# A hash-routed expert stage on one core: one flat loop over full tiles with copied weights, and slots of 40 rows for what is left

## The chip, the cores and the metric

One core of one Trainium2 chip runs the whole kernel. The metric is device time in microseconds (us) for one execution, lower is better. All arithmetic of the part that changes is float32.

## The reference, cut to what matters

2048 tokens (4 sequences of 512) of width 128 go through an attention block with a layernorm, and then through eight experts of hidden width 512. Which experts a token gets is a hash of its own first two values:

```python
h = jnp.mod(x_flat[:, :2].sum(axis=1).astype(jnp.int32), E)      # E = 8
sel = jnp.stack([h, jnp.mod(h + 1, E)], axis=1)
# for every expert e, and only for tokens with e in sel:
y = jnp.maximum(x_flat @ W1e + b1e, 0.0) @ W2e + b2e
acc += 0.5 * y
x = layernorm(x + acc)
```

So a token of group h needs experts h and h+1, and nothing else. With the inputs of setup_inputs, evaluating the reference's first half and its hash puts 1052, 324, 132, 35, 10, 29, 131 and 335 tokens into groups 0 to 7.

## The kernel before, in words

The core's engines are programmed one by one and meet through semaphores.

**Attention.** A loop over t = 0..18 (16 token tiles of 128 and a pipeline of three) computes attention on TensorE, ScalarE and VectorE. The normalised rows (x1, with the token's own index as a 129th value) are scattered by GpSimd's indirect DMA (line 514) into a DRAM array `groups`, in one segment for each group (`seg` in the code). In front of each segment lie 128 rows of padding whose index is out of range.

**Full tiles.** As soon as the first 12 token tiles are counted, VectorE computes on one row (full_tiles and full_rows, lines 920 to 944) the first FULL = 5 tiles that are certainly full, with their expert and start row (full_table). They run as five unrolled steps j = 0..4. SyncE reads their table entries into registers (load_table, line 306), and starts a DMA for the first-layer weights w1f (line 352, into a ring of three) and for the rows xrow (line 362). TensorE turns the rows (columns, line 1299), multiplies up (line 1308) and down (line 1323), ScalarE applies bias and relu (line 680, with biases b1x that VectorE picked) and copies the sum out (fsum, line 727). The second layer's weights are read from w2_s at an offset held in a register.

**Remaining tiles.** After the last tokens are placed, VectorE counts each group's remaining tiles (count_tiles, lines 956 to 971): at least one for each group. Then every engine runs eight loops, one for each group e, whose bounds come from tile_table. In each iteration k:
- SyncE waits for `kept` and `xT_up`, and fetches 128 rows twice: xs (line 387, to be turned) and xrow (line 388, for the residual).
- TensorE: up with expert e into bA (4 products of 128x128x128), up with expert e+1 into bB and bC (4 more), down with expert e (line 1452), the turn of the next tile's rows (columns, line 1303), down with expert e+1 (line 1459). Each float32 product is two instructions. Weights are read in place from w1_s and w2_s at fixed offsets.
- ScalarE: 4 relus for ha and 2 for hb (line 680). VectorE: the other 2 relus for hb (line 1077), the copy xsT (line 1051), the previous tile's finish (line 1045, which waits for the store before it), then ysum (1027), y2 (1032), bn_stats (1034) and bn_aggr (1037).
- GpSimd: the deviation (lines 557 and 559), the index copy (563) and the indirect store of the tile (567), one at a time: the copy waits until the store before it has landed.

A last tile of a group that is not full is run as a full tile of 128 rows, whose leading rows are done twice or are padding.

## Time and profile before

| | us |
|---|---|
| median of 3 runs | 238.8 (237.17 to 240.47) |
| the profiled execution, own time | 238.23 |
| its span in the trace | 236.5 |
| TensorE busy in the span | 212.2 (90%) |
| VectorE, ScalarE, GpSimd busy | 147.3, 120.6, 117.8 |

The profiled execution's own time is 1.73 us above its span: what lies around the traced instructions. Times in the rows below count from the span's start. "Idle before" names what ended an engine's wait. A chain of waits is followed back from the last instruction of the kernel.

### The profile page before, as it was taken

Reading aid. Unit: us, or ns where it says so; the run is one execution under the profiler, and the core shown is the slowest. Engines: PE = TensorE matmul, PEld = TensorE weight load, DVE = VectorE, ACT = ScalarE, POOL = GpSimd, SP = SyncE. Lnnn points to the kernel's source line nnn. Section 1 sums busy time; section 2 is a strip of 40 time slices with the busy share of each in tenths; the row PEclk is TensorE's granted clock in tenths of the full one; section 3 lists DMA queues with packets and bytes.
Section 4 is the critical chain, followed back from the end, with each engine's and each line's share of the span. In section 5 each row is a group of like instructions: output and inputs, shape, how many; then the busy total and the mean of one; then the engine's idle time right before and its main releaser. Section 6 shows DMA issues by size and latency. Waiting matters only on the chain.

```text
span 236.5 us, 10737 instructions
## 1 busy us (share of the span) xinstructions
PE 212.2 (90%) x4009; PEld 176.2 (75%) x4009; DVE 147.3 (62%) x521; ACT 120.6 (51%) x360; POOL 117.8 (50%) x219
## 2 busy tenths in 40 slices
PE   6879999999998999998999988999999999999920
PEld 2445778767777667886776678989999999899920
DVE  6836448585877765888898616734655555555540
ACT  3546557765466646765656145754344434344400
POOL 6563034852544427762647601847646545455541
PEclk9999999999999999999999999999999999999995
DMA  4131120112232132130001365212121212121100
GB/s 100 58 94 47 49 96 3 45 52 91 91 78 66 47 103 72 43 96 15 28 25 36 117 201 151 96 38 76 40 62 44 56 43 57 27 48 36 35 22 7
DMA packets 18557, 14.73 MB, mean 62 GB/s; under 512 B 2647, under 2 KB 15547, under 8 KB 18513
## 3 DMA queue, kind: packets, MB, share of 16 engines
q1 hardware_dynamic: 17008, 11.83, 17.9%
q0 software_dynamic: 1216, 2.16, 2.8%
q8 instruction: 30, 0.49, 0.9%
q10 hardware_dynamic: 288, 0.13, 0.3%
q14 instruction: 15, 0.11, 0.2%
HBM read 11.43 MB, written 3.03 MB: 61 GB/s over the span
## 4 chain that ended last, share of the span: by engine, by line
PE 74%; DVE 6%; issue 5%; DMA 4%; POOL 3%; ACT 3%; SPq 1%; POOLq 0%; ACTq 0%; DVEq 0%
PE bS L1308 12%; PE bT L1251 7%; PE bV L1452 6%; PE bV L1459 5%; PE bS L1194 4%; PE bV L1266 4%; PE bS L1219 4%; PE bJ L1170 3%; PE bV L1323 3%; PE bT L1308 3%; PE bS L1233 2%; PE bL L1367 2%; PE bS L1201 2%; PE bV L1274 2%; DMA out<-yo,idx 2%
## 5 line engine op out<-in xcount | busy, mean ns | idle before, releaser
L680 ACT ACTIVATE ha<-bS,b1c 128x128 f32<-128x128 f32 x68 | 19.4, 368 | 38.0 <-PE bS L1308 38.0
L668 ACT COPY PTs<-bT 128x512 f32<-128x512 f32 (+3 forms) x48 | 25.9, 539 | 18.2 <-PE bT L1251 18.2
L567 POOL DMA_INDIRECT out<-yo,idx x18 | 19.4, 1076 | 17.5 <-POOL idx L563 9.6
L1251 PE MATMUL bT<-ident,Pr 128*128 128x128 f32 x168 | 27.2, 277 | 0.5 <-issue 0.4
L1308 PE MATMUL bS<-xsT,w_s 128*128 128x128 f32 x204 | 26.3, 279 | 1.1 <-issue 1.0
L1308 PEld LDWEIGHTS bS<-xsT,w_s 128*128 128x128 f32 x204 | 24.1, 192 | 2.2 <-issue 2.2
L498 POOL TENSOR_SCALAR rstd<-mv 128x1 f32<-128x1 f32 x16 | 3.8, 236 | 44.0 <-DVE mv L859 44.0
L1251 PEld LDWEIGHTS bT<-ident,Pr 128*128 128x128 f32 x168 | 19.5, 141 | 5.4 <-issue 4.1
L514 POOL DMA_INDIRECT groups<-x,pos x16 | 16.5, 1034 | 11.7 <-DVE pos L909 8.4
L655 ACT ACTIVATE Pr<-bS 128x512 f32<-128x512 f32 x32 | 20.1, 629 | 3.0 <-PE bS L1233 3.0
L814 DVE TENSOR_REDUCE mx<-bS 128x8 bf16<-128x512 f32 x32 | 21.4, 677 | 0.0
L819 DVE TENSOR_REDUCE mx<-bS 128x8 bf16<-128x128 f32 (+3 forms) x16 | 7.9, 491 | 20.6 <-issue 14.9
L1459 PE MATMUL bV<-w_s,hb 128*128 128x128 f32 x136 | 18.5, 277 | 0.0
L1452 PE MATMUL bV<-w_s,ha 128*128 128x128 f32 x136 | 18.1, 276 | 0.2 <-DVE ysum L1027 0.2
L1077 DVE TENSOR_SCALAR hb<-bT,b1c 128x128 f32<-128x128 f32 x34 | 10.5, 347 | 11.7 <-PE bT L1308 11.0
L1459 PEld LDWEIGHTS bV<-w_s,hb 128*128 128x128 f32 x136 | 16.7, 191 | 0.3
L1452 PEld LDWEIGHTS bV<-w_s,ha 128*128 128x128 f32 x136 | 16.5, 192 | 0.4 <-ACT ha L680 0.4
L1266 PE MATMUL bV<-Vx,PTs 128*32 128x18 f32 x1024 | 15.2, 186 | 1.3 <-DVE rem L835 0.8
L1266 PEld LDWEIGHTS bV<-Vx,PTs 128*32 128x32 f32 x1024 | 12.4, 111 | 4.5 <-issue 3.2
L631 ACT COPY Vx<-bJ 64x256 f32<-64x256 f32 x32 | 12.0, 374 | 7.0 <-PE bJ L1170 6.8
L504 POOL TENSOR_SCALAR x<-y,mv,rstd 128x128 f32<-128x128 f32 x15 | 13.0, 867 | 1.6
L559 POOL TENSOR_TENSOR rstd<-rstd,half 128x1 f32<-128x1 f32 x22 | 12.5, 567 | 1.7
(237 smaller groups left out, 496.9 us busy)
## 6 DMA issues: line engine op xcount, KB each, us to landing
w_s<-in_L_ffn_W SPq DMA_DIRECT2D x16, 256.0 KB
w1f<-in_L_ffn_W SPq DMA_DIRECT2D x10, 256.0 KB, 3.0
xrow<-groups SPq DMA_DIRECT2D x22, 64.5 KB, 1.9
xs<-groups SPq DMA_DIRECT2D x18, 64.0 KB
x_tok<-in_L_attn_x SPq DMA_DIRECT2D x4, 256.0 KB, 3.7
groups<-padrows SPq DMA_DIRECT2D x1, 516.0 KB, 6.0
b2r<-in_L_ffn_b SPq DMA_DIRECT2D x1, 512.0 KB, 3.4
out<-yo,idx POOLq DMA_INDIRECT x18
```

Source lines behind the costliest of these rows:

```text
L504: nc.gpsimd.tensor_scalar(x1[:, t, 0:D], y[:, q, :], mv[:, q, 0:1], rstd[:, q, :], ALU.subtract, ALU.mult).then_inc(ln_done, 1)
L514: nc.gpsimd.indirect_dma_start(seg, bass.IndirectOffsetOnAxis(ap=pos[:, t:t + 1], axis=0), x1[:, t, :], None).then_inc(done, 16)
L567: nc.gpsimd.indirect_dma_start(rows_out, bass.IndirectOffsetOnAxis(ap=idx[:], axis=0), yo[:, FULL - 1, :], None, bounds_check=T * P - 1, o ...
L655: nc.scalar.activation(Pr[:, t % 2, j, :].rearrange("p (z c) -> p z c", z=2), own[j], ACT.Exp, scale=SCALE).then_inc(exped[j], 1)
L668: nc.scalar.copy(PTs[:, j, 0:m, :], bT[:, 0:m * P].rearrange("p (c q) -> p c q", c=m)).then_inc(turned_out, 1)
L680: nc.scalar.activation(dst[:, c, :], src[:, c * P:(c + 1) * P], ACT.Relu, bias=bias_of(c)).then_inc(relu, 1)
L814: nc.vector.tensor_reduce(mx[:, j, :].rearrange("p (z h) -> p z h", z=2), own[j].rearrange("p z (h k) -> p z h k", h=4), AX.X, ALU.max).th ...
L1251: last = nc.tensor.transpose(bT[:, c * P:(c + 1) * P], Pr[:, t % 2, j, c * P:(c + 1) * P], ident[:])
L1266: last = mm(bV[i * W:(i + 1) * W, a * PW:(a + 1) * PW], PTs[:, j, c, i * W:(i + 1) * W], Vx[:, q, i, a, :], start=True, stop=True)
L1308: last = mm(bank_of(c)[:, c * P:(c + 1) * P], w[:, c * P:(c + 1) * P], xsT[:], start=True, stop=True)
L1452: mm(bY[:, 0:D], ha[:, c, :], w2_s[:, e, c, :], start=(c == 0), stop=False)
L1459: last = mm(bY[:, 0:D], hb[:, c, :], w2_s[:, a, c, :], start=False, stop=(c == FC - 1))
```

## The change

A group's rest of up to TS = 40 rows is no longer a tile. Each group has a slot of 40 rows (its last 40), and three slots share one tile xt (GT = 3, TT = 3). Tiles beyond the five full ones are those that a group needs for all but such a rest. They run in one loop k = FULL..last on every engine, with expert and row read from a table in each iteration. TensorE reads its weights from four fixed buffers w1a, w1b, w2a and w2b; ScalarE copies the next tile's weights into them (128x512 float32 each). All of hb's relus move to VectorE. xb = 0.5 b2 + x is made ahead of the sum. The table (count_tiles) has an entry for each tile and is computed by a longer row of small VectorE operations on one partition; full_biases is gone and biases are read at an offset in a register. w1_s and w2_s have a ninth expert, a copy of the first.

After the loop come eight passes, one for each expert, in the order 1, 2, 3, 0, 4, 5, 6, 7: 80 columns (the slots of the two groups that use the expert) go up and down with weights of 64 columns, the sums gather transposed in three banks that begin with the second layer's biases, and are turned back, normalised and stored in three tiles of up to 120 rows.

At the end of attention the order on TensorE changes: the last token tile's turn (attT) is no longer behind columns(0) and up_full(0, 0). In SyncE's program, ahead of the loop's first fetch, stand now: eight table reads for the slots, two for the table, four DMAs of 256 KB for the first tile's weights, and eight DMAs for the slots' rows.

The diff, cut to its core:

```diff
+    TS = 40
+    GT = P // TS
+    TT = -(-E // GT)
+    LAST = (T * P + E * (P - TS - 1)) // P
+    NT2 = LAST - FULL
+    ENTRIES = NT2 + 1
+    SLOTS = LAST + 1
+    ORDER = [1, 2, 3, 0, 4, 5, 6, 7]
...
@@ SP @@
+                    if e <= E:
+                        sp.dma_start(w1_s[:, e, :], W1[e % E]).then_inc(f_in, 16)
+                        sp.dma_start(w2_s[:, e, :, :], W2[e % E].rearrange("(c p) d -> p c d", p=P)).then_inc(f_in, 16)
...
+            def load_tile(k, row):
+                sp.wait_ge(kept, k * 16)
+                sp.wait_ge(xT_up, k)
+                sp.dma_start(xs[:], seg[bass.ds(row, P), 0:D]).then_inc(tile_in, 16)
+                sp.dma_start(xrow[:, bass.ds(k * XW, XW)], seg[bass.ds(row, P), :]).then_inc(kept, 16)
+            tail = load_table(sp, tail_table, range(E), tails_ok, E * SEG - TS)
+            last = load_bound(sp)
+            e = load_table(sp, table[:, 0, :], [1], table_ok, E - 1)[0]
+            for s, w1_to, w2_to in ((0, w1a, w2a), (1, w1b, w2b)):
+                a = (e + s) % E
+                sp.dma_start(w1_to[:].unsqueeze(1),
+                             W1[bass.ds(a, 1)].rearrange("e p f -> p e f")).then_inc(first_in, 16)
+                sp.dma_start(w2_to[:].rearrange("p (c d) -> p c d", c=FC),
+                             W2[bass.ds(a, 1)].rearrange("e (c p) d -> p (e c) d", p=P)).then_inc(first_in, 16)
             sp.wait_ge(scattered_late, 16 * KT_)
-            for e in range(E):
-                if e > 0:
-                    tail += load_table(sp, tail_table, [e], tails_ok, E * SEG - P)
-                    first += load_table(sp, tile_table[:, 0, :], [e + 1], table_ok, T + E, FULL)
-                with sp.Fori(first[e], first[e + 1]) as k:
-                    i = nc.s_assert_within(k - first[e], 0, T - 1,
-                                           skip_runtime_bounds_check_because="a group has at most all T tiles")
-                    row = nc.s_assert_within(tail[e] - i * P, 0, E * SEG - P,
-                                             skip_runtime_bounds_check_because="rows of no token precede a group's")
-                    sp.wait_ge(kept, k * 16)
-                    sp.wait_ge(xT_up, k)
-                    sp.dma_start(xs[:], seg[bass.ds(row, P), 0:D]).then_inc(tile_in, 16)
-                    sp.dma_start(xrow[:, bass.ds(k * XW, XW)], seg[bass.ds(row, P), :]).then_inc(kept, 16)
-            sp.wait_ge(xT_up, first[E])
+            for g in range(E):
+                h = (g % GT) * TS
+                sp.dma_start(xt[h:h + TS, g // GT, :], seg[bass.ds(tail[g], TS), :]).then_inc(tail_in[g // GT], 16)
+            with sp.Fori(FULL, last) as k:
+                at = entry_of(k)
+                load_tile(k, sp.value_load(table[0:1, bass.ds(at, 1), 0:1].rearrange("a n c -> a (n c)"),
+                                           min_val=0, max_val=E * SEG - P))
+            sp.wait_ge(xT_up, last)
...
@@ GpSimd @@
+            tail_deviation(0)
+            pool.wait_ge(out_in, last * 16)
+            tail_deviation(1)
+            tail_store(0)
+            tail_deviation(2)
+            tail_store(1)
+            tail_store(2)
             pool.wait_ge(table_ok, 1)
-            pool.wait_ge(out_in, first[E] * 16)
+            pool.wait_ge(out_in, last * 16)
+            pool.wait_ge(tail_stored, 16 * TT)
...
@@ ScalarE @@
+            columns_copy(0)
+            act.wait_ge(b1c_ok, 1)
+            def bias_of(e):
+                return lambda c: b1c[:, bass.ds(e * FC + c, 1)]
+            def bias_at(e):
+                return lambda c: b1c[:, e * FC + c:e * FC + c + 1]
+            relus(ha, bA, 0, up_a, bias_of(experts[0]), FC)
...
+            for t in range(TT):
+                n = len(groups_of(t))
+                act.wait_ge(tail_up, t + 1)
+                nc.scalar.copy(xTt[:, t * GT:t * GT + n, :],
+                               slot_turn[t][:, 0:n * TS].rearrange("p (g r) -> p g r", g=n)).then_inc(tail_out, 1)
+            act.wait_ge(down, FULL)
+            nc.scalar.copy(fsum[:, HEAD, :], bY[:, 0:D]).then_inc(f_out, 1)
+            w1v = w1_s[:].rearrange("p e f -> p (e f)")
+            w2v = w2_s[:].rearrange("p e c d -> p (e c d)")
+            last = load_bound(act)
+            act.wait_ge(f_in, 32 * (E + 1))
+            with act.Fori(FULL, last) as k:
+                e, after = load_experts(act, k)
+                act.wait_ge(up_a, k + 1)
+                act.wait_ge(full_ok, 1)
+                for c in range(FC):
+                    nc.scalar.activation(ha[:, c, :], bA[:, c * P:(c + 1) * P], ACT.Relu,
+                                         bias=bias_of(e)(c)).then_inc(relu, 1)
+                act.wait_ge(full_ok, 1)
+                nc.scalar.copy(w1a[:], w1v[:, bass.ds(after * F, F)]).then_inc(w1a_ok, 1)
+                act.wait_ge(up_b, k + 1)
+                act.wait_ge(full_ok, 1)
+                nc.scalar.copy(w1b[:], w1v[:, bass.ds(after * F + F, F)]).then_inc(w1b_ok, 1)
+                act.wait_ge(half_down, k + 1)
+                act.wait_ge(full_ok, 1)
+                nc.scalar.copy(w2a[:], w2v[:, bass.ds(after * F, F)]).then_inc(w2a_ok, 1)
+                act.wait_ge(down, k + 1)
+                act.wait_ge(full_ok, 1)
+                nc.scalar.copy(w2b[:], w2v[:, bass.ds(after * F + F, F)]).then_inc(w2b_ok, 1)
+            for i, e in enumerate(ORDER):
+                h, src = slot_hidden[i % 3]
+                act.wait_ge(slot_up, i + 1)
+                if i >= 3:
+                    act.wait_ge(slot_down, i - 2)
+                for c in range(FC):
+                    nc.scalar.activation(h[:, c, 0:2 * TS], src[:, c * 2 * TS:(c + 1) * 2 * TS], ACT.Relu,
+                                         bias=bias_at(e)(c)).then_inc(slot_relu, 1)
...
@@ VectorE @@
+            with dve.Fori(HEAD, last1) as last:
+                k = last + 1
+                e = load_experts(dve, k)[0]
+                dve.wait_ge(up_b, k + 1)
+                dve.wait_ge(down, k)
+                for c in range(FC):
+                    nc.vector.tensor_scalar(hb[:, c, :], bB[:, c * P:(c + 1) * P],
+                                            b1c[:, bass.ds(e * FC + FC + c, 1)], 0.0, ALU.add, ALU.max).then_inc(relu_b, 1)
+                column_copy(k + 1)
+                dve.wait_ge(out_in, last * 16)
+                dve.wait_ge(rs_ok, k)
+                finish(FULL - 1)
+                dve.wait_ge(kept, k * 16 + 16)
+                dve.wait_ge(y_ok, k)
+                nc.vector.scalar_tensor_tensor(xb[:], b2f[:, bass.ds(e * D, D)], 0.5, xrow[:, bass.ds(k * XW, D)],
+                                               ALU.mult, ALU.add).then_inc(xb_ok, 1)
+                dve.wait_ge(down, k + 1)
+                dve.wait_ge(xb_ok, k + 1)
+                nc.vector.scalar_tensor_tensor(y2[:, FULL - 1, :], bL[:, 0:D], 0.5, xb[:], ALU.mult,
+                                               ALU.add).then_inc(y_ok, 1)
+                moments(k, FULL - 1)
...
+            tail_flatten(0)
+            tail_moments(0)
+            tail_finish(0)
+            tail_flatten(1)
+            tail_moments(1)
+            tail_flatten(2)
+            tail_moments(2)
+            tail_finish(1)
+            tail_finish(2)
...
@@ TensorE @@
-                if t == T + 2:
-                    keep_busy(6)
-                    columns(0)
-                    keep_busy(4)
-                    up_full(0, 0)
-                    pe.wait_ge(f_in, 32 * E)
-                    experts = load_table(pe, full_table[:, 0, :], [0, 1], full_ok, E - 1)
-                if t > T:
-                    keep_busy(6 if t == T + 1 else 2)
                 if t >= 3:
                     pe.wait_ge(gated, t - 2)
                     nc.tensor.transpose(aT, att[:], ident[:]).then_inc(attT_up, 1)
+                if t == T + 2:
+                    columns(0)
                 if t < T:
                     score_rows(t)
-                if t == T + 2:
-                    up_full(0, 1)
-                if t == T + 1:
+                if t >= T + 1:
...
+            pe.wait_ge(f_in, 32 * (E + 1))
+            experts = load_table(pe, experts1, [0, 1], full_ok, E - 1)
+            up_full(0, 0)
+            up_full(0, 1)
...
+            for t in range(TT):
+                n = len(groups_of(t)) * TS
+                pe.wait_ge(tail_in[t], 16 * len(groups_of(t)))
+                nc.tensor.transpose(slot_turn[t][:, 0:n], xt[0:n, t, 0:D], ident[0:n, 0:n]).then_inc(tail_up, 1)
+            pe.wait_ge(summed, T)
+            pe.wait_ge(first_in, 64)
+            with pe.Fori(FULL, last) as k:
+                pe.wait_ge(w1a_ok, k + 1)
+                up(lambda c: bA, k, w1a, up_a)
+                pe.wait_ge(w1b_ok, k + 1)
+                up(lambda c: bB, k, w1b, up_b)
+                pe.wait_ge(y_ok, k)
+                pe.wait_ge(w2a_ok, k + 1)
+                by_act = k * FC + FULL * FC
+                for c in range(FC):
+                    pe.wait_ge(relu, by_act + c + 1)
+                    i = mm(bL[:, 0:D], ha[:, c, :], w2a[:, c * P:(c + 1) * P], start=(c == 0), stop=False)
+                i.then_inc(half_down, 1)
+                columns(k + 1)
+                pe.wait_ge(w2b_ok, k + 1)
+                for c in range(FC):
+                    pe.wait_ge(relu_b, k * FC + c + 1)
+                    i = mm(bL[:, 0:D], hb[:, c, :], w2b[:, c * P:(c + 1) * P], start=False, stop=(c == FC - 1))
+                i.then_inc(down, 1)
+            HF = P // 2
...
+                dst = slot_hidden[i % 3][1]
+                if i >= 3:
+                    pe.wait_ge(slot_relu, FC * (i - 2))
+                if e == 0:
+                    cols = xTt[:, 0:E:E - 1, :]
+                else:
+                    cols = xTt[:, e - 1:e + 1, :].rearrange("p g r -> p (g r)")
+                for c in range(FC):
+                    for h in range(2):
+                        to = dst[h * HF:(h + 1) * HF, c * 2 * TS:(c + 1) * 2 * TS]
+                        last_up = mm(to.rearrange("p (g r) -> p g r", g=2) if e == 0 else to,
+                                     w1_s[:, e, c * P + h * HF:c * P + (h + 1) * HF], cols, start=True, stop=True)
+                last_up.then_inc(slot_up, 1)
...
+                groups = (0, E - 1) if e == 0 else (e - 1, e)
+                parts = [(groups[0], 0), (groups[1], 1)] if e % GT == 0 else [(groups[0], 0)]
+                for c in range(FC):
+                    pe.wait_ge(slot_relu, FC * i + c + 1)
+                    for g, q in parts:
+                        n = TS if len(parts) == 2 else 2 * TS
+                        at = (g % GT) * TS
+                        for h in range(2):
+                            last_down = mm(slot_sum[g // GT][h * HF:(h + 1) * HF, at:at + n],
+                                           w2_s[:, e, c, h * HF:(h + 1) * HF], hid[:, c, q * TS:q * TS + n],
+                                           start=False, stop=False, skip_group_check=True)
+                last_down.then_inc(slot_down, 1)
...
+            for i in range(E + 2):
+                if i < E:
+                    slot_pass_up(i)
+                if i >= 2:
+                    slot_pass_down(i - 2)
+                while back < TT and i - 3 >= max(ORDER.index((g + s) % E) for g in groups_of(back) for s in range(2)):
+                    turn_back(back)
+                    back += 1
```

## Rows read from the trace of the kernel before

**Rows 1.** The page: busy time of each engine.

```profile
PE 212.2 (90%) x4009; PEld 176.2 (75%) x4009; DVE 147.3 (62%) x521; ACT 120.6 (51%) x360; POOL 117.8 (50%) x219
```

**Rows 2.** Window from the loops' first to their last product: us, busy of each engine, clock.

```profile
159.70:226.40 66.70, 65.26 (x561) 63.34 (x560) 37.98 (x137) 28.14 (x102) 36.85 (x72) 1.00 0.19 47
```

**Rows 3.** The page: loop tiles' relus (four each).

```profile
L680 ACT ACTIVATE ha<-bS,b1c 128x128 f32<-128x128 f32 x68 | 19.4, 368 | 38.0 <-PE bS L1308 38.0
```

**Rows 4.** Chain of waits, loop tiles, TensorE: start us, us, what.

```profile
183.33 1.34 PE bS L1308 x12
...
187.01 1.34 PE bS L1308 x12
```

**Rows 5.** Timeline: TensorE's pair of table reads, the last token tile's sum, the first loop tile's turn.

```profile
138.91 0.39 PE L1281 MATMUL bJ<-spare 128*128 128x256 bf16 x2 [0.62 <-issue]
...
140.57 0.29 DVE L855 TENSOR_TENSOR y<-bL,x_tok 128x128 f32<-128x128 f32 x1 [4.43 <-PE bL L1367]
...
157.97 0.27 PE L1303 MATMUL bS<-ident,xs 128*128 128x128 f32 x1
```

**Rows 6.** Timeline of SyncE's DMA issues before the loops and at the first tile.

```profile
143.26 3.23 SPq L352 DMA_DIRECT2D w1f<-in_L_ffn_W  x4
153.96 0.33 SPq L387 DMA_DIRECT2D xs<-groups  x1
154.50 0.35 SPq L388 DMA_DIRECT2D xrow<-groups  x1
```

**Rows 7.** Chain of waits: SyncE's table reads ahead of its first DMAs, and a landing.

```profile
130.83 0.47 SPq L306
...
132.16 0.02 SPq L306
...
133.86 2.48 DMA xrow<-groups
```

**Rows 8.** Timeline of VectorE: a turn of the loop without, then one with a table read.

```profile
173.55 0.18 DVE L1037 BATCH_NORM_AGGREGATE mv<-st 128x2 f32<-128x6 f32 x1
...
174.04 0.61 DVE L1077 TENSOR_SCALAR hb<-bT,b1c 128x128 f32<-128x128 f32 x2 [0.30 <-issue]
...
196.36 0.18 DVE L1037 BATCH_NORM_AGGREGATE mv<-st 128x2 f32<-128x6 f32 x1
197.46 0.61 DVE L1077 TENSOR_SCALAR hb<-bT,b1c 128x128 f32<-128x128 f32 x2 [0.92 <-PE bT L1308]
197.98 0.28 DVE L1051 COPY xsT<-bS 128x128 f32<-128x128 f32 x1
198.18 0.34 DVE L1045 TENSOR_SCALAR yo<-y,mv,rstd 128x128 f32<-128x128 f32 x1
...
199.26 0.29 DVE L1032 SCALAR_TENSOR_TENSOR y<-ysum,xrow 128x128 f32<-128x128 f32 x1
199.58 0.29 DVE L1034 BATCH_NORM_STATS2 st<-y 128x6 f32<-128x128 f32 x1
```

**Rows 9.** Timeline of ScalarE: two 128x512 operations in a row; the relus of a loop tile.

```profile
124.47 0.63 ACT L655 ACTIVATE Pr<-bS 128x512 f32<-128x512 f32 x1
...
124.96 0.63 ACT L659 ACTIVATE Pr<-bS 128x512 f32<-128x512 f32 x1
...
184.26 1.14 ACT L680 ACTIVATE ha<-bS,b1c 128x128 f32<-128x128 f32 x4 [2.03 <-PE bS L1308]
```

**Rows 10.** Timeline: weight loads of 128 and of 32 columns, and products on the latter.

```profile
122.32 0.71 PE L1170 MATMUL bJ<-wvg,xT 128*32 128x64 f32 x32 [0.28 <-ACT ranks L623]
...
122.78 0.43 PEld L1266 LDWEIGHTS bV<-Vx,PTs 128*32 128x32 f32 x32
...
181.16 0.97 PEld L1452 LDWEIGHTS bV<-w_s,ha 128*128 128x128 f32 x8
```

**Rows 11.** Timeline: last products and last store of the kernel.

```profile
225.27 1.06 PE L1459 MATMUL bV<-w_s,hb 128*128 128x128 f32 x8
...
230.59 1.05 POOL L567 DMA_INDIRECT out<-yo,idx  x1 [0.85 <-POOL idx L563]
```

More of the change, by code:

```diff
@@ L306, in load_table, with load_bound, entry_of, load_experts @@
             return [eng.value_load(tab[0:1, i:i + 1], min_val=least, max_val=most) for i in entries]
+        rows1, experts1 = table1[:, 0, :], table1[:, 1, :]
+        def load_bound(eng):
+            return load_table(eng, bound_table, [0], table_ok, LAST, FULL + 1)[0]
+        def entry_of(k):
+            return nc.s_assert_within(k - FULL, 0, NT2 - 1,
+                                      skip_runtime_bounds_check_because="the loop ends at the table's last entry")
+        def load_experts(eng, k):
+            at = entry_of(k)
+            return [eng.value_load(table[0:1, bass.ds(at, 1), i:i + 1].rearrange("a n c -> a (n c)"),
+                                   min_val=0, max_val=E - 1) for i in (1, 2)]
+        def groups_of(t):
+            return range(t * GT, min((t + 1) * GT, E))
         def expand(eng, dst, src, mask, n):
@@ L701, in _ @@
                 if t == T + 1:
-                    columns_copy(0)
+                    for s in (w1a_ok, w1b_ok, w2a_ok, w2b_ok):
+                        act.sem_inc(s, FULL + 1)
+                    act.sem_inc(half_down, FULL)
+                    experts = load_table(act, experts1, [0, 1], full_ok, E - 1)
                 if 1 <= t <= T:
@@ L727, in _ @@
                     nc.scalar.copy(fsum[:, j, :], bY[:, 0:D]).then_inc(f_out, 1)
[L728 removed]
+            relus(hb, bB, HEAD, up_b, bias_of(experts[HEAD] + 1), FC // 2)
             columns_copy(FULL)
[L730 to L740 removed]
+            relus(hb, bB, HEAD, up_b, bias_of(experts[HEAD] + 1), FC, FC // 2)
@@ L956, in count_tiles @@
[L956 to L970 removed]
+                n = FULL
@@ new lines, in full_rows @@
+                ends = spread(upto[:, Z + 1:], n)
+                row, expert = found1[:, 0, :], found1[:, 1, :]
+                link(nc.vector.tensor_tensor(reached[:, 0:n, :], ends, along(0, n), ALU.is_le))
+                nc.vector.tensor_reduce(expert, reached[:, 0:n, 0:E - 1], AX.X, ALU.add)
+                link(nc.vector.tensor_tensor(cover[:, 0:n, :], reached[:, 0:n, :], ends, ALU.mult))
+                link(nc.vector.tensor_reduce(gone[:], cover[:, 0:n, :], AX.X, ALU.max))
+                link(nc.vector.scalar_tensor_tensor(row, gone[:], -float(P), jrow[:, 1, 0:n], ALU.mult, ALU.add))
@@ new lines, in _ @@
+            pe.wait_ge(b2q_in, 16)
+            pe.wait_ge(share_ok, 1)
+            pe.wait_ge(f_out, FULL)
+            pe.wait_ge(tail_out, TT)
+            for t in range(TT):
+                slot_biases(t)
+            pe.wait_ge(xT_out, last + 1)
+            back = 0
+            for i in range(E + 2):
[6 more added lines that the diff above has]
+                    back += 1
```

383 lines of the change are left out of this document (213 added, 170 removed).

## The prediction

> **What bounds the kernel now.** I read the page's busy times first: TensorE is busy for 90% of the span, nobody else for over 62% [rows 1]. Then the stretch that the change rewrites, the loops over the remaining tiles. It is 66.7 us long, TensorE is busy for 65.3 us of it at the full granted clock (1.00, the 2.4 GHz level), ScalarE for only 28.1 us and VectorE for 38.0 us [rows 2]. So the loops are TensorE's. How many tiles? ScalarE does 68 relus into ha, four for each tile: 17 tiles [rows 3]. 66.7 / 17 = 3.92 us each. In the chain of waits one undisturbed tile follows the other after 187.01 - 183.33 = 3.68 us [rows 4]; the 0.24 us on top are turns of loops and changes of expert.
>
> **What the change removes.** By the reference the groups hold 1052, 324, 132, 35, 10, 29, 131 and 335 tokens. Five full tiles come from group 0. Before, the rest needs 4+3+2+1+1+1+2+3 = 17 tiles, which the trace bears out. After, a group needs ceil((n-40)/128) tiles in all: 3+3+1+0+0+0+1+3 = 11 in the loop. Six tiles go, 6 x 3.92 = 23.5 us. Four things pay for that, in the order of time.
>
> **Step A: the loop starts later.** In the five unrolled steps TensorE turns the first loop tile's rows inside the last step, at 157.97, and the loops start 1.73 us later, at 159.70 [rows 2, 5]. After the change TensorE gets to the last token tile's projection before it multiplies the first full tile, which brings that tile's sum (140.57 [rows 5]) some 3 us forward, and with it the placing. But SyncE's program decides when the rows of the first loop tile come, and SyncE works without a pause there: the last four DMAs of full-tile weights end at 143.26 + 3.23 = 146.5 [rows 6]. Behind them now stand:
> - ten table reads. Two of SyncE's take from 130.83 to 132.18, 1.35 us [rows 7]; TensorE does a pair in 0.62 us [rows 5]. I take 0.6 us for one, nearer to SyncE's own row: 6.0 us, with 3.1 and 6.8 us as ends;
> - four DMAs of 256 KB, at most 3.23 / 4 = 0.8 us each, of which part is table reads; I take 0.6: 2.4 us;
> - eight slot DMAs, each at the pitch of two neighbours, 154.50 - 153.96 = 0.54 us [rows 6]: 4.3 us;
> - one more table read for the tile's row, 0.6 us, and the landing: a fetch of the same size took 2.48 us on the chain [rows 7], I take 2.2.
> Sum: 146.5 + 6.0 + 2.4 + 4.3 + 0.6 + 2.2 = 162.0, and 0.5 for the loop's entry and the waits: 162.5. TensorE would be ready for it near 156, so it stands idle for over 6 us, and all small savings ahead of it (the earlier last tile, full_biases gone, register offsets for relus that are slower) fall into that hole and are worth nothing. The static part ends at 162.5 + 1.7 = 164.2. Ends: 161 and 166.
>
> **Step B: a tile of the flat loop.** TensorE still has the same 32 instructions and one turn, 3.68 us at least. Two others now have more than that.
> - VectorE. From the start of hb's two relus to xsT it takes 0.52 us, so 0.26 for one [rows 8]; four are 1.04. xsT to yo is 0.20; yo, then xb, then y2 0.44 each way as from one 128x128 operation with a semaphore to the next (estimate from yo's own 0.34 and the 0.1 around it): 0.85. y2 to bn_stats is 0.32 [rows 8], to bn_aggr 0.40. From bn_aggr to the next relu a plain turn takes 174.04 - 173.55 = 0.49 us, one with a table read and a change of loop 197.46 - 196.36 = 1.10 [rows 8], so a read costs up to 0.6; with two reads in each turn I take 1.5. Sum: 1.04 + 0.20 + 0.85 + 0.32 + 0.40 + 1.5 = 4.31 us.
> - ScalarE. Four relus 1.14 [rows 9]. A copy of 128x512 from SBUF is not in the trace; the nearest rows, from PSUM, take 0.63 each and start 0.49 apart [rows 9], so four are 1.96 to 2.5. The last copy waits for the tile's last product; from there 1.5 us for turn and reads (as for VectorE, part of it beside the copy), 1.14 of relus, 0.3 until the first half's last pair is through, 1.0 for the turn and the second half: 4.0 to 4.1 us from product to product.
> I take 4.3 us, VectorE's sum; 3.92 (TensorE's mean of before) and 5.15 are the ends, the latter worked out below. Entry: TensorE turns the slots, ScalarE copies them (three times), copies fsum, reads the bound and the first entry before the first relu: 1.4 us more than in a steady turn. 164.2 + 1.4 + 11 x 4.3 = 212.9.
>
> **Step C: the slots' passes.** Each product of float32 is two instructions. Up: 8 passes x 4 x 2 halves x 2 = 128. Down: five passes of 16 and three (experts 0, 3, 6, whose two slots lie in different banks) of 32 = 176. Together 304, with weights of 64 columns. Weight loads of 128 columns come 0.97 / 8 = 0.121 us apart, those of 32 columns, in turn over four column strips, 0.43 / 32 = 0.013; products of 64 columns on the latter 0.71 / 32 = 0.022 [rows 10]. There is no row for 64 columns. Two strips side by side and 80 columns to move make some 0.035, nearest to the strips' rows: 304 x 0.035 = 10.6 us; with the biases' products and the fill 11.4. Ends: ScalarE's 32 relus at 0.25 each and the first pass make 10 us whatever TensorE does; at 0.055, halfway in columns, it is 17.5; at the 0.11 of whole weights 34.
>
> The Trainium skill speaks against this part: "TensorE: Matmul & The Clock Gate", section "LDWEIGHTS (loading the stationary operand)", gives a load its columns divided by 1.2 in ns. For 128 columns that is 107 ns, and this trace agrees (121). For 32 it would be 27 ns, and this trace shows 13, so strips load side by side here. By the rule alone, 53 ns for 64 columns, the passes would take 304 x 0.053 = 16.1 us and more, and the forecast would be some 5 us longer (an estimate from that page).
>
> **Step D: the end.** Before, the last products end at 226.33, the last store is issued at 230.59 and the span ends at 236.5: 10.2 us, of which 5.9 lie behind the store's issue [rows 11]. After, the turn of slot tile 1, its moments, the flattening of tile 2, its turn and moments, its deviation on GpSimd, and two stores in a row (1.05 us each) stand between the last product and the last store: 5.1 us instead of 4.3. With 5.9 behind: 11.0. Ends: 10.2 and 12.
>
> **The sum.** 212.9 + 11.4 + 11.0 = 235.3 us of span, against 236.5. The profiled execution took 1.73 us more than its span: 237.0 us. Its own 238.23 was 0.6 below the runs' median of 238.8, within their spread. So: six tiles (-23.5) are paid with +4.5 at the start, +1.4 at the entry, 11 x 0.38 = +4.2 in the loop, +11.4 for the passes and +0.8 at the end: -1.2 us. Forecast: no change that can be told from none (within 2%, 234.0 to 243.6), 237.0 us, own range 233 to 243.
>
> **Rivals.**
> 1. The gain comes through. The turn's table reads hide beside the engines' work (in the plain turn VectorE loses only 0.30 us), so that the tile stays TensorE's 3.92, and SyncE reads as fast as TensorE does (0.31), which takes 2.9 us off step A: 237.0 - 11 x 0.38 - 2.9 = 229.9 us. For it: ScalarE idles 38 us behind products in the loops of before, so there is room [rows 3]. Against it: VectorE's turn with one read was late against its product (idle 0.92, of which the plain turn explains half).
> 2. ScalarE becomes the loop's bound and the kernel slower. It has relus 1.14, four copies of 0.63 without overlap 2.52, two reads and a turn 1.5, of which nothing is hidden if it cannot run ahead of waiting copies: 5.15 us. 11 x 0.85 = 9.4 more: 246.4 us. It decides from 4.9 us per tile on, where 243.6 is passed. For it: each copy waits for a product, and each operand has an offset in a register, for which no ScalarE row exists. Against it: the back-to-back pitch of 0.49.
> 3. The 64-column weights don't run side by side. At 0.055 us per instruction step C costs 6 us more, 243 us, from 0.057 on the kernel is slower by over 2%, at 0.11 it takes 259 us. For it: the whole-weight row; against it: the strips' rows. The rule of the Trainium skill weighed at step C describes this case.
> 4. The tile count doesn't fall to 11. Rows 3 confirm the counts that give 17, so I give this next to nothing.
>
> **Chances.** Forecast (within 2%) 0.40. Rival 1 and mixtures of its two parts 0.36. Rival 2 0.12, rival 3 0.12, both slower by over 2%. The range takes in rival 1 and reaches rival 2's beginning: 229 to 246.
>
> **What would show it.** Right: ScalarE has 44 relus into ha in the loop (11 tiles); TensorE is idle for 5 us or more behind a DMA into xs before the loop; xs is issued near 160; tiles follow after 4.2 to 4.5 us with VectorE late; the passes' weight loads come some 0.035 us apart; the last store is issued about 5 us behind the last product. Wrong: xs issued before 157 (step A), a tile period under 4 or over 4.9 us (step B), passes of under 10 or over 16 us (step C). The whole is wrong above all if SyncE's reads are cheap or if the turn of a loop costs ScalarE what it costs nobody in the trace of before.

## The result and the profile after

The changed kernel takes 245.52 us (median of 4 runs, 244.49 to 246.50) against 238.64 us for the one before on the same chip: ratio 1.026 with a 95% interval of 1.021 to 1.031, so it is slower by more than 2%. The forecast was no change at 237.0 us. The time lies above the forecast's own range (233 to 243) and just inside the wide one with the rivals (229 to 246), at the place where the second rival begins. Ratios, here and below, leave out every execution that took over 1.5% longer than the fastest of the same kernel. The profiled execution took 246.5 us with a span of 244.5.

The page's part 1 of the changed kernel (busy time, share of the span, instructions), to be held against [rows 1]:

```profile
PE 212.9 (87%) x4113; PEld 173.1 (71%) x4113; DVE 144.1 (59%) x520; ACT 137.2 (56%) x383; POOL 112.3 (46%) x208
```

TensorE is busy as long as before (212.2 us there). The passes take 11.3 us of it, the 11 tiles 48.7 us (4.4 each, against 65.3 / 17 = 3.8 before, since products that are slowed by their input or run at half rate count as busy), and 5.3 us more than before lie ahead of the loop. No other engine is at its limit by this line, and yet two of them set the time of a tile. The groups of the loop show it (busy, mean ns | idle before, and what ended it):

```profile
L1227 DVE TENSOR_SCALAR hb<-bS,b1c 128x128 f32<-128x128 f32 x44 | 12.4, 344 | 21.2 <-PE bS L1498 18.8
L861 ACT ACTIVATE ha<-bS,b1c 128x128 f32<-128x128 f32 x44 | 12.6, 368 | 14.6 <-PE bS L1498 14.6
L1632 PE MATMUL bL<-w2a,ha 128*128 128x128 f32 x88 | 13.7, 299 | 3.4 <-ACT ha L861 3.4
```

44 relus into ha, four for each tile, answer to the 68 of [rows 3]: 11 tiles, as worked out. The names behind "<-" mislead in the first two lines: VectorE and ScalarE seem to wait 18.8 and 14.6 us for TensorE's first-layer product. But in the tile told below L1498's two groups end at 203.72 and 204.62, and the relus start at 204.53 and 205.51: the products were there 0.8 and 0.9 us earlier, and the sequencers were still turning the loop and reading the table. The last line is the honest one: TensorE waits for ScalarE's relus.

The same points before and after (us from the span's start):

| | before | after |
|---|---|---|
| last token tile's sum | 140.57 [rows 5] | 141.86 |
| first product of the loops | 159.70 [rows 2] | 168.06 |
| last product of the loops | 226.33 [rows 11] | 221.2 |
| last product of the experts | 226.33 | 232.6 |
| last store issued | 230.59 [rows 11] | 238.90 |
| end of the span | 236.5 | 244.5 |

**The entry.** The timeline of SyncE's DMA issues before the loop, answering to [rows 6]:

```profile
147.21 2.78 SPq L417 DMA_DIRECT2D w1f<-in_L_ffn_W  x4
156.45 0.33 SPq L449 DMA_DIRECT2D w1a<-in_L_ffn_W  x1
...
158.51 3.65 SPq L456 DMA_DIRECT2D xt<-groups  x8
163.41 0.37 SPq L441 DMA_DIRECT2D xs<-groups  x1
```

The chain of waits where SyncE's ten table reads begin (L353 is a read):

```profile
149.98 0.43 DVE tail_table L1099
150.43 0.27 SPq L353
```

And TensorE's timeline at the same place:

```profile
158.91 1.06 PE L1498 MATMUL bS<-xsT,w1f 128*128 128x128 f32 x8
159.80 1.11 PE L1513 MATMUL bV<-w_s,ha 128*128 x8
165.33 0.48 PE L1493 MATMUL bS<-ident,xs 128*128 128x128 f32 x1 [4.42 <-DMA xs<-groups]
165.60 2.13 PE L1513 MATMUL bV<-w_s,hb 128*128 x8
...
168.06 1.99 PE L1498 MATMUL bS<-xsT,w1a 128*128 128x128 f32 x8
```

From the last full-tile weights' DMA (it ends at 149.99) SyncE needs 13.4 us to the issue of xs: 0.4 until VectorE has written the table of the slots' rows, 6.0 for ten reads (150.43 to 156.45), and the rest for the DMA issues, one more read and the loop's entry. TensorE stands idle for 4.42 us, and the eight products behind the wait take 2.13 us where eight took 1.06 to 1.11 before it: half the rate. The windows (from:to us, busy of each engine, granted clock, DMA share, GB/s) say that it is the clock:

```profile
150.00:160.00 10.00, 10.00 (x92) 10.00 (x91) 7.66 (x38) 6.89 (x27) 5.43 (x9) 1.00 0.49 146
160.00:165.00 5.00, 0.91 (x8) 0.72 (x7) 1.40 (x6) 0.63 (x2) 4.23 (x7) 0.94 0.56 157
165.00:168.00 3.00, 2.67 (x12) 2.53 (x13) 0.00 (x0) 0.83 (x4) 0.34 (x1) 0.50 0.34 83
```

1.00 while TensorE is busy, then 4.4 us without work, then 0.50, the 1.2 GHz level, when the work is back.

**A tile of the loop.** The chain of waits (start us, us, what; ACTq is ScalarE's sequencer, L366 the table read):

```profile
201.66 0.91 PE bL L1638 x8
...
202.66 0.05 ACT w2b L873
...
203.08 0.28 ACTq L366
...
203.77 0.28 ACTq L366
...
204.53 0.38 ACT ha L861
204.91 0.04 issue
204.95 1.26 PE bL L1632 x8
206.22 0.11 PE bS L1493
```

The second half of the second layer ends, the copy of w2b that waited for it starts, the loop turns, two reads follow 0.69 us apart, the first relu comes 1.87 us behind the copy, and only then may TensorE multiply. L1638 started at 201.66 and starts again 4.66 us later, at 206.32; the tiles beside it take 4.67 us, where [rows 4] had 3.68.

**The passes and the end.** Some groups of TensorE's timeline in the passes, then GpSimd's of the last stores:

```profile
224.23 0.72 PE L1656 MATMUL bS<-xTt,w_s 128*64 128x80 f32 x16
224.79 0.72 PE L1672 MATMUL bS<-hb,w_s 128*64 128x80 f32 x16
...
231.84 0.75 PE L1672 MATMUL bT<-hb,w_s 128*64 128x80 f32 x16
```

```profile
235.30 1.07 POOL L684 DMA_INDIRECT out<-yot,xt  x1 [0.33 <-issue]
236.38 0.23 POOL L675 TENSOR_TENSOR rstd2t<-mv2t,half 80x1 f32<-80x1 f32 x1
236.69 0.57 POOL L677 TENSOR_TENSOR rstd2t<-rstd2t,half 80x1 f32<-80x1 f32 x1
...
238.90 0.94 POOL L684 DMA_INDIRECT out<-yot,xt  x1 [0.30 <-issue]
```

Groups of 16 with 64-column weights start 0.56 us apart, 0.035 us each. The third slot tile's deviation (rstd2t) stands behind the first one's store on GpSimd, although its input was ready at 235.43.

### The profile page after: what moved, and what is told of

It is laid out like the page before. It is cut to its first block, busy times and chain, and to the rows that moved or that the text cites. A ratio compares the mean times of both kernels' runs of the same rounds, so it can differ in the third digit from the quotient of the medians.

```text
span 244.5 us, 11108 instructions
## 1 busy us (share of the span) xinstructions
PE 212.9 (87%) x4113; PEld 173.1 (71%) x4113; DVE 144.1 (59%) x520; ACT 137.2 (56%) x383; POOL 112.3 (46%) x208
## 4 chain that ended last, share of the span: by engine, by line
PE 62%; issue 10%; DVE 6%; SPq 5%; ACTq 5%; ACT 5%; DMA 2%; POOL 2%; DVEq 1%; POOLq 0%
PE bT L1441 7%; PE bL L1632 5%; PE bL L1638 4%; PE bS L1384 4%; PE bV L1456 4%; ACTq L366 4%; PE bS L1409 3%; PE bJ L1360 3%; PE bL L1548 2%; SPq L353 2%; PE bV L1464 2%; PE bS L1423 2%; PE bS L1391 2%; PE bS L1656 2%; PE bV L1513 2%
## 5 line engine op out<-in xcount | busy, mean ns | idle before, releaser
L1227 DVE TENSOR_SCALAR hb<-bS,b1c 128x128 f32<-128x128 f32 x44 | 12.4, 344 | 21.2 <-PE bS L1498 18.8
L649 POOL DMA_INDIRECT out<-yo,idx x12 | 12.6, 1050 | 21.1 <-DVE yo L1193 20.2
L861 ACT ACTIVATE ha<-bS,b1c 128x128 f32<-128x128 f32 x44 | 12.6, 368 | 14.6 <-PE bS L1498 14.6
L1632 PE MATMUL bL<-w2a,ha 128*128 128x128 f32 x88 | 13.7, 299 | 3.4 <-ACT ha L861 3.4
L1632 PEld LDWEIGHTS bL<-w2a,ha 128*128 128x128 f32 x88 | 11.7, 188 | 5.3 <-ACT ha L861 5.3
L1360 PE MATMUL bJ<-wvg,xT 128*32 128x64 f32 (+1 forms) x512 | 12.6, 228 | 2.8 <-issue 2.4
L1498 PE MATMUL bS<-xsT,w1a 128*128 128x128 f32 x88 | 13.3, 297 | 0.4
L1498 PEld LDWEIGHTS bS<-xsT,w1a 128*128 128x128 f32 x88 | 11.5, 204 | 2.0 <-issue 2.0
L374 POOL TENSOR_TENSOR Kx<-KT,slot 128x512 f32<-128x512 f32 x12 | 12.4, 1036 | 0.0
L1638 PE MATMUL bL<-w2b,hb 128*128 128x128 f32 x88 | 11.8, 277 | 0.7 <-DVE hb L1227 0.7
```

What stands on the lines that cost most here:

```text
L649: nc.gpsimd.indirect_dma_start(rows_out, bass.IndirectOffsetOnAxis(ap=idx[:], axis=0), yo[:, FULL - 1, :], None, bounds_check=T * P - 1, o ...
L1360: last = mm(bJ[r * W:(r + 1) * W, at:at + wide], xT[:, b % 2, w:w + W], wvg[:, c, 0:wide], start=True, stop=True)
L1498: last = mm(bank_of(c)[:, c * P:(c + 1) * P], w[:, c * P:(c + 1) * P], xsT[:], start=True, stop=True)
L1632: i = mm(bL[:, 0:D], ha[:, c, :], w2a[:, c * P:(c + 1) * P], start=(c == 0), stop=False)
L1638: i = mm(bL[:, 0:D], hb[:, c, :], w2b[:, c * P:(c + 1) * P], start=False, stop=(c == FC - 1))
```

## The experiments

The first eight kernels below ran on a second chip, where the kernel before takes 247 us, the third profile of before and SyncE's order alone on another (237.5), the moved store and the last version on one more (238.3). So each is compared with the runs of the kernel before beside it, and otherwise by stretches of its own trace.

**The rows of the first loop tile, ahead of the slots.** SyncE's order (the four weights' DMAs, the slots' reads and the slots' DMAs follow where the dots are), and the slots' turns and copies moved behind the loop:

```diff
+row = load_table(sp, table[:, 0, :], [0], table_ok, E * SEG - P)[0]
+sp.wait_ge(scattered_late, 16 * KT_)
+load_tile(FULL, row)
...
-with sp.Fori(FULL, last) as k:
+with sp.Fori(FULL + 1, last) as k:
```

> Edit: SyncE fetches the first loop tile's rows (after three table reads) before the weights' four DMAs, the eight slot reads and the eight slot DMAs; the slots' turns and their copies move behind the loop. Theory (step A, the queue of SyncE): xs is issued near 154 instead of 163.4, TensorE idles for under 1 us instead of 4.6 us and its granted clock stays at the upper level there, so the loop starts 5 to 7 us earlier; the slots' turns and copies add about 1 us behind it: 240 us, ratio to the changed kernel near 0.977. Rival (the hole is only moved): the weights of the first loop tile or the last scatter end just as late, and under 2 us are won.

Ratio 1.039 (1.031 to 1.048), worse. Its waits of SyncE, and TensorE's timeline at the second tile:

```profile
SPq L440 <- PE bS L1492: 4.8, 1, 4.8
```

```profile
183.38 0.47 PE L1496 MATMUL bS<-ident,xs 128*128 128x128 f32 x1 [2.85 <-DMA xs<-groups]
```

The hole moved: TensorE waits 1.78 us for the first tile's weights (from 174.20 to 175.98), and then for the second tile's rows. The first line shows one more thing: load_tile begins with a wait until all five static tiles are turned, so that xs, though issued first in the program, was not issued before 168.35.

**The two engines' share in a tile.** On ScalarE, w2b is copied for the tile in hand behind its relus, so that no copy stands between the last product and the turn (the DMA that filled w2b ahead of the loop goes too):

```diff
-act.wait_ge(down, k + 1)
-nc.scalar.copy(w2b[:], w2v[:, bass.ds(after * F + F, F)])
...
+act.wait_ge(down, k)
+nc.scalar.copy(w2b[:], w2v[:, bass.ds(e * F + F, F)])
```

> Edit: ScalarE copies w2b for the tile in hand, behind its relus, instead of for the next tile behind the tile's last product; its two table reads so begin before the tile ends. Theory: the turn of ScalarE's loop and its reads (1.75 us) leave the chain, and VectorE's own round (2.8 us of work and 1.7 us of turn and reads) bounds the tile next: 4.5 us instead of 4.67, 2 us in all. Rival: VectorE's reads run beside other work too, then the tile falls to 3.9 us and 8 us are won. Second rival: ScalarE reads late all the same, 4.67 stays.

On VectorE, the second table read, whose value it never uses, is left out:

```diff
-e = load_experts(dve, k)[0]
+e = load_experts(dve, k, (1,))[0]
```

> Edit: VectorE reads one table entry in a turn instead of two (the second was never used). Theory (ScalarE's chain bounds the tile): no change, 4.67 us. Rival (VectorE's sum of step B bounds it): 0.5 to 0.7 us less for each of 11 tiles, 6 to 8 us.

And both:

> Both edits, ScalarE's shift and VectorE's single read. Theory: with both chains shorter the tile takes 3.9 to 4.0 us, 7 to 8 us less than the changed kernel in all, far more than the sum of the two alone. Rival (the copies themselves, 2.5 us, or TensorE bound it elsewhere): 4.3 us or more stay.

The shifted copy alone: ratio 1.016 (1.009 to 1.024), 4.66 us for a tile. The single read alone: 1.018 (1.006 to 1.031), 4.67 us. Both: 0.993 (0.989 to 0.998), 4.08 us. With the shifted copy alone the chain runs over VectorE's own reads, with the single read alone over ScalarE's as before. With both it holds nothing but TensorE:

```profile
199.71 0.93 PE bL L1634 x8
200.63 0.11 PE bS L1495
200.74 1.14 PE bL L1640 x8
201.88 1.92 PE bS L1500 x16
```

So two chains of equal length (4.67 and 4.66 us) bound a tile, and either edit alone is worth nothing. Together they give 0.59 x 11 = 6.5 us. TensorE's 4.08 us are still more than its 3.68 of [rows 4]: its second half (L1640) takes 1.14 us where it took 0.89, and its weight load waits 0.22 us for VectorE's hb.

**One read more on ScalarE.**

```diff
-e, after = load_experts(act, k)
+e, after, _ = load_experts(act, k, (1, 2, 1))
```

> The changed kernel with one more table read on ScalarE in every loop tile (its value is not used). Theory (ScalarE's turn, reads, relus and copies bound the tile): a tile takes 4.67 + 0.6 to 0.7 = 5.3 to 5.4 us, 7 to 8 us more over 11 tiles. Rival (something else sets 4.67, and ScalarE has room): 4.67 stays.

TensorE's timeline:

```profile
197.90 1.26 PE L1632 MATMUL bL<-w2a,ha 128*128 128x128 f32 x8 [1.15 <-ACT ha L861]
...
203.11 1.26 PE L1632 MATMUL bL<-w2a,ha 128*128 128x128 f32 x8 [1.14 <-ACT ha L861]
```

5.21 to 5.24 us a tile, 0.55 us more for one read of a register: a little less than expected, and no sign of room. The single time, 257.11 us, is 5.9 above the unchanged copy's median beside it (251.26); 11 x 0.55 are 6.1.

**The changed kernel and the one before, again.**

> The changed kernel as it is, beside the others on one chip. Ratio to before near 1.026; loop tiles 4.67 us apart; SyncE's first DMA into xs about 13 us behind the last w1f DMA; TensorE idle over 2 us ahead of that tile. If the ratio is under 1.01, much of the loss measured first was the chip's or the run's.

> The kernel before, profiled once more on this chip, for the attention part. Theory (the change delays the attention part itself, by its code or its ninth pair of weights): from the residual sum near 101 us to the one near 133 us this kernel takes about 32 us again, as in its first profile, against 34 to 40 in the profiles with the change. Rival (TensorE stalls of 1.6 to 2.7 us in that stretch fall on either kernel, by the run or the chip): it takes 36 us or more here too, and its chain has such a stall.

The changed kernel: 251.26 us (median of all four executions), ratio 1.014 (1.004 to 1.024), tiles 4.68 us apart. SyncE's first DMA into xs is issued 14.4 us behind the last w1f DMA, for about 13 expected. The expected wait for xs is missing: in this profile (the longest of the four executions, 253.76 us) ScalarE stood still for 3.03 us inside the static part, with nothing on this core in the trace that released it, and TensorE came to the turn after the rows had landed. From the last static up product to the loop's first it took 3.7 us there, against 168.06 - 158.91 = 9.15 in the first profile. So part of the entry's price is hidden here, which may be why the ratio is smaller; that is not shown, and the two intervals only just overlap.

The kernel before took 140.65 - 101.94 = 38.7 us between the two residual sums, like the seven others on that chip (37.5 to 40.3), against 31.9 in its first profile. Its chain:

```profile
114.38 0.29 DVE loc L831
114.67 0.13 another core or an unknown queue
114.80 2.28 issue
117.08 0.09 DVE mx L819
```

The stall of 2.28 us is VectorE's, not TensorE's as I had it in the theory, and all seven others on that chip have one of 2.3 to 2.4 us at the same place. It is a third of the 6.8 us; the rest is open.

**The kernel before, a third time**, because in its first profile there was no stall near 102 us, while the changed kernel's had one of 1.80 us (at 103.33):

> The kernel before, profiled a third time. Theory (TensorE's stalls of 1.7 to 2.3 us in the attention part belong to the chip and the run): where this chip is the one on which the others show such a stall near 102 us, this kernel shows one too, and takes 33 to 34 us from the residual sum near 101 us to the one near 133 us. Rival (the change adds one stall of about 2 us there, its code lying differently): this kernel takes 31.9 us again, or 2 us less than the kernels with the change on the same chip.

```profile
100.99 0.41 PE bJ L1170 x20
101.40 1.95 issue
103.35 0.26 PE bJ L1170 x3
```

It has TensorE's stall too, in the middle of a group of products that wait for nothing, and 34.8 us from sum to sum (135.28 - 100.53). The changed kernel with SyncE's order alone, told below, ran on the same chip, has none there and takes 132.12 - 100.46 = 31.7 us. These stalls of TensorE fall on either kernel; they aren't the change's.

**SyncE's order with slot reads first, together with the two loop edits.** The weights' DMAs stand between the two tiles' rows, the slots' DMAs behind them:

```diff
 tail = load_table(sp, tail_table, range(E), tails_ok, E * SEG - TS)
+row = load_table(sp, table[:, 0, :], [0], table_ok, E * SEG - P)[0]
+sp.wait_ge(scattered_late, 16 * KT_)
+load_tile(FULL, row)
...
+load_tile(FULL + 1, row)
...
-with sp.Fori(FULL, last) as k:
+with sp.Fori(FULL + 2, last) as k:
```

> The variant in which w2b is copied behind the relus and VectorE reads one entry (it ran at 4.08 us a tile), and with it SyncE in a new order: 8 slot reads, then the first loop tile's rows as soon as the last scatter has landed, then the weights, then the second tile's rows, then the slots' 8 DMAs, the slots' turns and copies behind the loop. Theory (the static part waits for SyncE's issues, not for the scatter): the first DMA into xs is issued about 9 us behind the last w1f DMA rather than 13, TensorE's wait of 2 to 4.4 us ahead of the tile is gone and no tile behind it waits; some 1 us comes back behind the loop for the turns: 1.5 to 3.5 us less than that variant, ratio to before 0.978 to 0.988. Rival (the hole only moves, to the second or third tile or behind the loop): ratio 0.99 to 1.00, with a wait for a DMA of 1.5 us or more at another place.

Ratio 0.993 (0.983 to 1.002), no better than without. SyncE's waits and TensorE's timeline:

```profile
SPq L440 <- PE bS L1496: 4.4, 1, 4.4
```

```profile
170.60 2.05 PE L1505 MATMUL bS<-xsT,w1a 128*128 128x128 f32 x8 [2.39 <-DMA w1b<-in_L_ffn_W]
```

The wait for xs is gone and one of 2.39 us for the first tile's weights has come. SyncE stood 4.4 us at load_tile's wait for the turns, with the weights' DMAs behind it. The static tiles are turned from xrow, not from xs, so the first loop tile needs no such wait.

**That wait left out, and one store moved.** First the store alone, on the changed kernel:

```diff
 tail_deviation(0)
-pool.wait_ge(out_in, last * 16)
-tail_deviation(1)
 tail_store(0)
+pool.wait_ge(out_in, last * 16)
+tail_deviation(1)
 tail_deviation(2)
```

> The changed kernel with one store moved on GpSimd: the first slot tile's store is issued ahead of the second's deviation, not behind it, so that the third's deviation doesn't queue behind it. Theory (the last store is late because rstd2t of the third slot tile waits for that store's issue): from the last product (TensorE's last pass, 231.84 + 0.75 in the changed kernel's profile) to the issue of the last store 5.3 to 5.6 us instead of 6.3 to 6.5. Rival (the chain of turn, sum, moments sets it alone): 6.3 to 6.5 again.

From the end of the last product (229.25 + 0.75 = 230.00) to the last store's issue at 235.48 it takes 5.5 us; the changed kernel takes 238.90 - 232.59 = 6.3. So 0.8 us of the end was that queue on GpSimd.

```profile
229.25 0.75 PE L1672 MATMUL bT<-hb,w_s 128*64 128x80 f32 x16
```

```profile
235.48 0.93 POOL L684 DMA_INDIRECT out<-yot,xt  x1 [0.31 <-issue]
```

Nine profiles with the store in its old place take 6.1 to 6.3 us there; the last version below, with the store moved, takes 5.2.

Then SyncE's order alone: slot reads, weights' DMAs, first tile's rows without the wait, second tile's rows, slots' DMAs; the loop as it was.

```diff
-sp.wait_ge(xT_up, k)
+if turned is None:
+    sp.wait_ge(xT_up, k)
...
-load_tile(FULL, row)
+load_tile(FULL, row, 0)
```

> The changed kernel with nothing but SyncE's new order (weights, first tile's rows without the wait for the turns, second tile's rows, slots' DMAs; slots' turns behind the loop); the loop is left as it was. Theory (entry and loop are separate prices that add): no wait for a DMA into xs, from the last static first-layer product (L1498's last group) to the loop's first about 3 to 4 us instead of 8, loop tiles 4.67 us; 4 to 5 us less than the changed kernel, ratio to before 1.00 to 1.01. Rival (ScalarE's chain starts the loop late in any case, so that the rows' earlier landing gains little without the loop's edits): 0 to 2 us less, ratio 1.015 to 1.025.

241.37 us against 237.46 beside it, ratio 1.017 (1.004 to 1.030): the runs alone tell neither theory from the other. The profile does. From the last static up product (155.21) to the loop's first (160.28) it takes 5.1 us instead of 9.15, the tiles stay 4.67 us apart, and of the wait 1.34 us is left, which I had expected to be gone:

```profile
158.56 0.33 PE L1499 MATMUL bS<-ident,xs 128*128 128x128 f32 x1 [1.34 <-DMA xs<-groups]
```

The DMA into xs, issued at 154.64 with four DMAs of 256 KB just ahead of it, took 3.88 us to land, against 1.87 in the first profile. That its place behind them is the reason is argued, not tried.

At last everything together.

> All together: w2b's copy behind the relus, one read on VectorE, the slot store of tail_order, and SyncE in the order 8 slot reads, first loop tile's weights, its rows (which no longer wait for the static tiles' turns, since those don't use xs), second tile's rows, slots' DMAs; slots' turns behind the loop. Theory (the entry's hole was SyncE's order and that one wait for the turns): neither a DMA into xs nor one into the weights holds TensorE for over 0.3 us before the first loop tile, tiles 4.08 us apart, 1.5 to 2.5 us less than the two loop edits alone (ratio 0.993 there), with the tail's 0.9: ratio to before 0.973 to 0.987. Rival (the static part and the attention part give it back, or the slots' rows are late behind the loop): 0.988 to 1.0.

232.51 us, ratio to the kernel before beside it 0.977 (0.972 to 0.983): faster than it by 1.7 to 2.8%. The changed kernel itself did not run on that chip; with only its store moved it took 243.08 us once. TensorE's timeline at the entry, and the chain of a tile:

```profile
157.62 1.10 PE L1521 MATMUL bV<-w_s,ha 128*128 x8
158.66 0.33 PE L1501 MATMUL bS<-ident,xs 128*128 128x128 f32 x1
...
160.38 1.13 PE L1506 MATMUL bS<-xsT,w1a 128*128 128x128 f32 x8
```

```profile
184.67 0.92 PE bL L1635 x8
185.59 0.11 PE bS L1501
185.70 1.14 PE bL L1641 x8
186.84 1.86 PE bS L1506 x16
```

TensorE waits for no DMA (0.93 us is left for ScalarE's relus in the first tile) and never runs at half rate there, and from the fourth tile on a tile takes 4.03 us. The store's variant ran beside it: its span is 241.1 us, this one's 230.1. The difference of 11.0 us comes out of parts: 11 x (4.67 - 4.03) = 7.0 in the loop, 8.9 - 3.7 = 5.2 at the entry, less 1.0 for the slots' turns behind the loop: 11.2.

## Why the prediction was wrong

Its own sum was 235.3 us of span; 244.5 came. Two steps failed, the turn with two table reads in step B and the starting point of step A. The 9.2 us, by its steps:

- **The tiles removed**: 17 to 11, right.
- **Step A**, +3.5 us. The sum for SyncE's run was right: 16.0 us from the last weights' DMA to the landed rows were forecast, 15.3 came, and ten reads took the 6.0 us forecast. Wrong was its starting point, "the last four DMAs of full-tile weights end at 143.26 + 3.23 = 146.5": they ended at 149.99. That was taken over from the profile of before, and in this run the attention part was later. A stall of TensorE (1.80 us at 103.33) makes up about half of that, and such stalls fall on either kernel (the third profile of before has one at the same place); the rest is not accounted for. Where no such stall fell, with SyncE's order alone, these DMAs ended at 146.29, and the last token tile's sum came at 136.97, 3.6 us ahead of [rows 5], where some 3 us were forecast. With SyncE's order as in the changed kernel and a stall of 1.68 us (the profile of the moved store) they ended at 147.24. So most of this part belongs to the run, not to the kernel. The other 0.7 is the last static products at half the rate behind the wait, 2.4 us instead of 1.7: I had named the idle stretch and costed what follows it at full clock. What I hadn't seen is that the hole (4.42 us here, for over 6 forecast) is the order of SyncE's issues, and that a better order is worth little while load_tile's wait for the turns stands in it.
- **Step B**, +4.8 us, the largest part. The step failed where it says "with two reads in each turn I take 1.5", "from there 1.5 us for turn and reads" and "I take 4.3 us, VectorE's sum". On VectorE the 1.5 us were counted from bn_aggr's start; from there to the next hb it took 205.51 - 203.45 = 2.06 us, 0.56 more, while yo to y2 took 0.65 instead of 0.85. On ScalarE it took 204.53 - 202.57 = 1.96 us from the last product to the first relu, 0.46 more, and the first half of the second layer is paced by the relus: 1.26 + 0.42 us from first relu to its end instead of the 1.44 worked out. So both have 4.66 to 4.67 us, not 4.31 and not 4.0 to 4.1. The mechanism is half the forecast's (VectorE's round) and half rival 2's (ScalarE's, at 4.67 instead of 5.15): on neither engine are the reads hidden. The extra read (0.55 us a tile) and the pair of edits (0.59 us only together) show it. 11 x 0.37 = 4.1 us. The other 0.7 lies in the entry, which has 6.7 us from the static part's end (167.73) to the end of the first tile's products (174.47), for 5.7 forecast, 0.37 of it the tile's own. The chain runs there over the slots' copies, fsum, VectorE's last static sum and its three table reads to hb at 172.80, not over the half rate. By itself 4.67 lies under the 4.9 that I gave as the point of decision: without step A's 3.5 us the time would have been 242.0 us, inside the forecast's 2%.
- **Step C**, right: 11.4 us (221.22 to 232.59) for 11.4 forecast, 0.035 us for an instruction as taken. By the rule of the Trainium skill, "TensorE: Matmul & The Clock Gate", section "LDWEIGHTS (loading the stationary operand)", 64 columns would be 53 ns; this trace shows 35, and the rival that followed the rule is out. There was no row for 64 columns, so that 0.035 came true to the digit is partly luck.
- **Step D**, +0.9 us: 6.3 us from the last product to the last store's issue for 5.1 forecast, and 5.6 behind it for 5.9. The mis-sized term is the queue on GpSimd, where the third deviation stands behind a store of 1.07 us; the prediction had listed both and counted them as if side by side. The moved store gives 0.8 back.
- Its own signs: 44 relus and 0.035 us came. TensorE's idle stretch was 4.42 us instead of 5 or more, xs was issued at 163.41 instead of near 160, tiles came 4.67 us apart instead of 4.2 to 4.5, and the last store 6.3 us behind the last product instead of about 5.
- Chances: slower had 0.24, as two single mechanisms. That three misses of 1 to 5 us add up in the same direction wasn't among the cases, and that was the way to this result. That 245.5 us lies in the wide range at all is no merit of the sum.

What stays open: what the stalls are. TensorE has one near 102 us (1.7 to 2.2 us) in four profiles, one of them of the kernel before, and VectorE one near 115 us (2.3 to 2.4 us) in all eight profiles on the second chip, the kernel before among them. ScalarE has one of 1.8 to 3.1 us ahead of its second copy into fsum, in all seven versions with the change on the second chip and in none elsewhere; the kernel before stands still for 1.91 us right behind that copy there. They have no releaser on this core in the trace, and no run here was made to tell their cause.

## What to carry to other kernels

When a straight-line or multi-loop schedule is turned into one flat loop, count what every sequencer does between its last wait and its first instruction: turn and table reads stand on the path of each engine that waits for the last product, and the page's idle column puts them down to somebody else. Where two engines have the same turn, mend both before judging either. A helper that carries a wait carries it also to the place where it isn't needed.

## What the runs showed of the hardware

- A table entry read into a register costs 0.55 us as an additional read on ScalarE, 0.69 from one read to the next on the chain, 0.6 on SyncE (ten in 6.0 us); TensorE did two in 0.62 [rows 5]. A turn of the loop with two reads costs VectorE 1.88 us from the end of one tile's last operation to the next tile's first, and ScalarE 1.87 us from the start of its last copy.
- A copy of 128x512 float32 from SBUF on ScalarE takes 0.62 to 0.64 us, and neighbours start 0.51 apart.
- After 4.42 us without work eight products took 2.13 us instead of 1.06: a wait in front of a dense stretch costs more than its length. The same came after waits of 4.13 us (2.13 us, in the profile of the moved store) and 2.39 us (2.05 us, at a granted clock of 0.50), and not after 1.34 us (the granted clock stayed at 1.00).
- TensorE stops for 1.7 to 2.2 us within a group of products that wait for nothing, in the kernel before too (1.95 at 101.40); VectorE stops for 2.28 us at 114.80, and ScalarE for 1.8 to 3.1 us ahead of one copy, with nothing on this core that releases them. Two profiles of the kernel before, on two chips, differ by 6.8 us in a stretch of five token tiles, as much as the change moved.
